# Head attention on one core: in the last step of a pair, the second head's row maximum moves ahead of the reciprocal and the scaling of v

## The reference

```python
q = jnp.einsum('bsd,hpd->bhsp', x, q_w) + q_b      # 16 heads of 64
k = jnp.einsum('bsd,hpd->bhsp', x, k_w) + k_b
v = jnp.einsum('bsd,hpd->bhsp', x, v_w) + v_b
scores = jnp.einsum('bhqp,bhkp->bhqk', q, k) / jnp.sqrt(jnp.float32(P))
attn = jax.nn.softmax(scores, axis=2)
ctx = jnp.einsum('bhqk,bhkp->bqhp', attn, v)
out = concat @ l_w.T + l_b
```

## Time and profile before

| | |
|---|---|
| runs | 1457.03 us median of 3 (1456.51 to 1458.73) |
| the profiled execution's own time | 1458.3 us |
| its span | 1456.6 us |
| granted TensorE clock | 0.999 of full speed |
| PE busy | 1424.7 us (98%) |
| DVE busy | 1069.7 us (73%) |
| ACT busy | 918.2 us (63%) |
| POOL busy | 279.7 us (19%) |

### The profile page before, as it was taken

How to read it: one execution, slowest core, us unless ns; L and a number is a source line. 1 busy time by engine, 2 the same in 40 slices (tenths; PEclk the granted TensorE clock), 3 DMA queues, 4 the chain that set the end, 5 groups by cost and what they waited for, 6 DMA issues and landing times.

```text
span 1456.6 us, 43343 instructions
## 1 busy us (share of the span) xinstructions
PE 1424.7 (98%) x18426; PEld 1023.6 (70%) x18426; DVE 1069.7 (73%) x2172; ACT 918.2 (63%) x1727; POOL 279.7 (19%) x325
## 2 busy tenths in 40 slices
PE   7999989999999999999999999999999999999997
PEld 6989954656777665667777756577777566777487
DVE  6885168987676678887666788876667887787764
ACT  5775766666666666666666666666666666666544
POOL 5166713022110022120000121300000213000046
PEclk9999999999999999999999999999999999999999
DMA  7502311011000111010000110100101111101002
GB/s 223 205 19 61 93 48 48 17 29 47 22 19 16 35 29 32 26 44 17 16 17 16 43 31 23 44 24 16 31 16 40 31 26 34 34 16 31 2 19 59
DMA packets 44464, 58.30 MB, mean 40 GB/s; under 512 B 8231, under 2 KB 32656, under 8 KB 44144
## 3 DMA queue, kind: packets, MB, share of 16 engines
q1 hardware_dynamic: 35120, 38.27, 9.5%
q0 software_dynamic: 9152, 17.26, 4.4%
HBM read 22.14 MB, written 19.32 MB: 28 GB/s over the span
## 4 chain that ended last, share of the span: by engine, by line
PE 87%; DVE 5%; issue 3%; POOL 2%; ACT 2%; DMA 1%; POOLq 0%; DVEq 0%; ACTq 0%
PE bank L1134 30%; PE bank L1147 29%; PE bank L1057 6%; PE bank L1062 4%; PE bank L1071 3%; PE bank L1289 2%; PE bank L1285 2%; PE bank L1246 1%; PE bank L406 1%; PE bank L434 1%; DVE stats L1330 1%; PE bank L811 1%; PE bank L815 1%; PE bank L803 1%; POOL xslots L651 1%
## 5 line engine op out<-in xcount | busy, mean ns | idle before, releaser
L1178 ACT ACTIVATE prob<-bank,nmx 128x1024 f32<-128x1024 f32 x512 | 570.3, 1114 | 418.2 <-DVE nmx L1169 416.8
L1169 DVE TENSOR_REDUCE nmx<-bank 128x1 f32<-128x1024 f32 x512 | 626.4, 1224 | 202.3 <-PE bank L1134 183.7
L1147 PE MATMUL bank<-prob,vsc 64*64 64x512 f32 x4096 | 644.3, 590 | 1.4 <-DVE ctxT L1196 0.7
L1134 PE MATMUL bank<-q,k 64*64 64x512 f32 x2048 | 526.9, 592 | 3.0 <-ACT prob L1178 1.9
L1134 PE MATMUL bank<-q,ks 64*64 64x512 f32 x2048 | 525.5, 590 | 0.0
L1147 PEld LDWEIGHTS bank<-prob,vsc 64*64 64x64 f32 x4096 | 240.7, 133 | 116.1 <-issue 41.5
L1057 PE MATMUL bank<-xT,wqkv_sb 64*64 64x256 f32 (+1 forms) x1560 | 213.0, 435 | 0.0
L1134 PEld LDWEIGHTS bank<-q,ks 64*64 64x64 f32 x2048 | 138.3, 133 | 77.9 <-issue 18.5
L1741 POOL DMA_INDIRECT yg<-yslots,row_ring x64 | 64.6, 1010 | 604.6 <-PE bank L1134 579.2
L1134 PEld LDWEIGHTS bank<-q,k 64*64 64x64 f32 x2048 | 134.3, 133 | 32.3 <-ACT prob L1178 7.4
L1057 PEld LDWEIGHTS bank<-xT,wqkv_sb 64*64 64x64 f32 x1560 | 93.5, 133 | 86.5 <-issue 34.4
(11 more groups left out here) (270 smaller groups left out, 1596.0 us busy)
## 6 DMA issues: line engine op xcount, KB each, us to landing
ks<-k SPq DMA_DIRECT2D x62, 256.0 KB, 3.1
yslots<-slots_sb SPq DMA_DIRECT2D x7, 640.0 KB, 3.6
slots_sb<-xslots SPq DMA_DIRECT2D x5, 640.0 KB, 4.6
xslots<-xhat_r POOLq DMA_DIRECT2D x5, 512.0 KB, 7.1
yslots<-xhat_r POOLq DMA_DIRECT2D x5, 512.0 KB, 12.3
w_sb<-in_w SPq DMA_DIRECT2D x1, 2048.0 KB, 9.3
wqkv_sb<-in_wqkv SPq DMA_DIRECT2D x1, 2048.0 KB, 18.8
xslots<-xhat_r,row_s POOLq DMA_INDIRECT x112
```

What stands on the lines that cost most here:

```text
L1134: ins = nc.tensor.matmul(bank[rows(c), SC[h][n], :], kk[r, cols(2 * j + c, HD)], qst[pi % 2][r, cols(n, HALF)], start=True, stop=True)
L1147: ins = nc.tensor.matmul(bank[rows(h), CX[n], :], vsc[s][rows(r), rows(h)], prob[g % 3][h][rows(r), cols(n, HALF)], start=(j == 0 and firs ...
L1169: nc.vector.tensor_reduce(nmx[:, 2 * s + h:2 * s + h + 1], bank[:, SC[h][0]:SC[h][0] + 2, :], mybir.AxisListType.XY, ALU.max, negate=True) ...
L1178: nc.scalar.activation(prob[g % 3][h][:].rearrange("p (n c) -> p n c", c=HALF), bank[:, SC[h][0]:SC[h][0] + 2, :], ACT.Exp, bias=nmx[:, 2 ...
```

## The change

In the DVE list of a step with j = 7, the maximum of the second head of step g + 2 now stands ahead of the reciprocal and the scaling of v of step g + 1. It is so in 31 of the 256 steps (g = 7, 15, ..., 247; the last pair's last step makes no scores and scales nothing). The other steps, the other engines and the computation stay as they are.

```diff
                 pi, j = g // T, g % T
                 if g < LAST - 1:
                     score_max(v, g + 2, 0)
-                if g < LAST:
+                if g < LAST and j < T - 1:
                     scale_v(v, step, g + 1)
                 if g < LAST - 1:
                     score_max(v, g + 2, 1)
+                if g < LAST and j == T - 1:
+                    scale_v(v, step, g + 1)
                 side_vector(v, step, g)
                 if j in (4, 5) and pi < NPAIRS - 1:
                     v_evac(v, pi + 1, j, pj_bank(g))
```

## The result

| | before | changed |
|---|---|---|
| median, 9 runs each | 1458.18 us | 1461.95 us |
| ratio, 95% interval | | 1.0024 (1.0015 to 1.0033) |
| span of the profiled execution | 1456.6 us | 1459.5 us |
| granted TensorE clock | 0.999 | 0.999 |
| PE / DVE / ACT busy | 1424.7 / 1069.7 / 918.2 us | 1424.8 / 1068.3 / 919.0 us |

By the ratio the changed kernel is slower by 3.5 us (2.2 to 4.8); 3.3 were forecast. The ratio isn't the quotient of the two medians, which lie 3.8 us apart here. The busy times of PE, DVE and ACT differ by 1.4 us at most, and DVE's fell, so what was added is waiting. From the first maximum of g = 7 to that of g = 247 it takes 1113.45 us before and 1116.77 us after: 3.32 us more inside the stretch that the change touches.

A forecast was written before the change was run, and what follows sets the result against it. PE was taken to bound the kernel, with 87% of the chain against DVE's 5%. Terms 3.36 - 0.3 + 0.2 gave 3.3 us more, the median going from 1457.0 to 1460.3 us; range 1457.9 to 1462.0 us.

The forecast's parts named there:

- the eight: Boundaries with side work, no DVE idle time and PE already waiting for the copy: 0.42 us each, 3.36 us more.
- the three in between: g = 15, 231, 239, where PE arrives 0.15 to 0.3 after the copy: 0.2 us more together.
- s = 31: g = 31, 95, 159: scores end earlier, so the second maximum starts 0.10 earlier; 0.3 us gained.
- the eleven: Boundaries where PE has a longer expert or router piece ahead of its last context product: cost 0.
- The second maximum gains nothing at 28 places: At places like g = 135 the second head's scores hold its maximum, not the scaling: gain 0.
- faster: Rival: the scaling holds the second maximum, which could start earlier at some 20 boundaries; 3 us gained, 1454.0 us; chance 0.03.
- The pair costs 0.42: Reciprocal and scaling, moved between second maximum and copy, add 0.42 us to DVE's work there, not 0.48.
- partly absorbed: Rival: PE or DVE wins back half of the loss at the eight; 1.6 us more, 1458.6 us; chance 0.17.
- the six plain boundaries: Boundaries without side work, like g = 191: the exponential still holds the upper half's scores; cost 0, uncovered 1.8 us.
- The lower half doesn't count: PE's upper half sets the pace; the rival that the lower counts too gives 1463.0 us, chance 0.10.

The follow-up runs named there:

- e1: Moved order only at g = 7, 23, 55, 71, 87, 135, 151, 199, against the kernel before: 1461.74 us against 1458.34, ratio 1.0022.
- e4: Changed order plus a spare, unused reciprocal and scaling behind the scaling, against the kernel before: 1469.53 us against 1458.34, ratio 1.0074.
- e2: Moved order only at the other 23 of the 31 boundaries, against the kernel before: 1458.82 us against 1458.34, ratio 1.0002.
- e9: Last step's side work behind copy and output addition, moved order only at g = 31, 95, 159, against the kernel before: 1456.53 us against 1458.79.
- e5: Order of before, last step's side work behind copy and output addition, against the kernel before on a slower chip: ratio 0.9990.
- e7: e5 plus the moved order at g = 31, 95 and 159, against the kernel before on a slower chip: ratio 1.0002.
- c0: Control: the kernel before, unchanged, run on a third chip, against the kernel before: ratio 1.0002.

## Why the prediction was right

It was right in direction, place and mechanism, and in the size of the difference: 3.3 forecast, 3.32 inside the stretch, 3.5 by the timing. The closeness of the sums is partly luck: the eight gave 0.13 less than forecast, and the three in between, s = 31 and the eleven together 0.2 more. Luck is also that the changed kernel's own median, 1461.95 us, lies inside the stated 1457.9 to 1462.0, by 0.05: the forecast of 1460.3 started from a median of 1457.0 over three runs, and over nine runs before took 1458.18.

Step by step:

- *The second maximum gains nothing at 28 places.* It started 1.72 after the first in all of them, now with 0.49 us of idle time ahead where the pair stood. Hence the rival "faster" is out: DVE's start followed the recorded end of the scores with the pair and without it.
- *The pair costs 0.42.* It was 0.40; the statistics and the copy start that much after the reciprocal. The 0.48, from the reciprocal's start to the scaling's recorded end, would have been further off: the statistics at 843.83 start 0.08 before that end at 843.91. The prediction took it as what follows from the page "VectorE: DVE Perf Modes" of the Trainium skill (The DRAIN you can't avoid), by which the next operation waits until the pipe is empty. The same paragraph of the page adds that an operation that isn't held starts earlier, and the 0.08 here fits that addition.
- *Eight places pay in full.* 3.23 us; e1 has them alone, e4 doubles them to 0.80 each. Nothing was absorbed on the way to the next boundary, and so the rival "partly absorbed" is out.
- *The exponential covers the six plain boundaries.* Shown twice: free in e2, 0.18 of the upper half each in e4, when the copy outlasts it. The copy came 0.24 to 0.25 later there, not 0.42 at most or about 0.3.
- *s = 31 gains 0.3.* 0.26, 0.28 in e9, and 0.24 between e5 and e7; only the boundaries can tell it.
- *Three in between, 0.2.* This term was mis-sized: 0.30, of which 0.21 at g = 15, where the upper half came only 0.05 later and the lower 0.16.
- *The lower half doesn't count.* True for what the change did at the six plain boundaries, 0 at all of them, where the lower half's delay is gone a step later. As a rule it is too simple. A delay or a gain of the lower half that lasts up to router work on PE is taken on by the upper half there. At g = 119, one of the eleven, the lower half is 0.05 later and the upper 0.00, until the piece of line 1246 in g = 124: then both are 0.04 later. At g = 231 and 239 the lower half stays 0.16 later over the whole stretch, no such piece follows, and the stretches pay the upper half's 0.05 and 0.04 alone. e9's eight gains follow the same rule. At g = 15, whose own step has a piece of line 1269, the upper half's scores are 0.05 later at the boundary and from the next step on 0.21, like the lower half's, though that step has no such piece itself. The rule is read from these timelines; no run isolated it, and what passes the lead on stays open.

The page "TensorE: Matmul & The Clock Gate" of the Trainium skill (The mechanism) has matmuls start and end in program order. The traces here don't agree: in each of the 256 steps, in every run, the second head's first q,k on the upper half starts before the second q,ks on the lower half, which stands ahead of it (in e2 at g = 191 1109.87 against 1110.96). Had the q,k waited for that q,ks, the six plain boundaries could not have been free in e2. So "nothing reorders it", said ahead of the prediction, is true of the lists and not of the starts on PE's two halves.

## What to carry to other kernels

Work that fills a wait of an in-order engine is free where it stands. Moved behind the instruction that had to wait, it lengthens the run up to the next handover (0.40 us at the eight places), and the instruction that moves ahead is no earlier, if another engine had held it. So look first at what ends the wait of the instruction that is to move ahead (a start right after the other engine's end, with idle time in front), and then at which instruction behind it has someone waiting. Here the gain lay in the opposite direction: the side work moved behind the copy that PE waits for (e9, 1.8 us less than before).

## What the hardware showed beyond that

- Three executions of the same instructions in this stage repeat each other to 0.02 us at every boundary (before, c0 and the untouched places of e1), while the spans of before and c0 differ by 1.5 us through what happens ahead of it. Distances between marks inside the stage can tell 0.1 us; the span and the timing can't tell 1.
- The two halves of PE's array run as two streams with a lead of one over the other. A delay of the leading one by up to 0.24 us was free at the boundaries without side work (g = 215 in e2), one of the other was counted in full (0.40 at the eight). Where the leading one's delay or gain lasted up to router work on PE, it was counted too (0.25 in e9; 0.21 at g = 15).
- One chip took some 2% longer for the kernel before (1486.9 against 1458.3 and 1458.8 us) and for the four that ran beside it. In e5's trace from it the granted clock was 0.93 in the second 100 us and PE was busy for 87.1 us of them, where c0 on another chip had 1.00 and 95.9 us.
